# Non-local attention in a four-stage fp32 kernel: which operand of the weighting matmul is held in the array, and how the rows' sums are divided out

## What is computed

```python
s = xf * gate                                  # 256 channels x L
theta, phi, g = (w @ s + b for three 1x1 convolutions)   # 128 x L each
attn = softmax(einsum("nci,ncj->nij", theta, phi), axis=-1)   # L x L
nl = einsum("ncj,nij->nci", g, attn)           # 128 x L
out = s + out_w @ nl + out_b
```

## Time and profile before

| | us |
|---|---|
| median of 3 runs | 7601.4 |
| the profiled execution's own time | 7604.33 |
| its span, first to last instruction | 7602.3 |
| PE busy (matmuls) | 6744.9 |
| DVE busy | 6281.6 |
| ACT busy | 5777.6 |
| POOL busy | 5368.3 |

### The profile page before, as it was taken

How to read it: one execution, slowest core, us unless ns; L and a number is a source line. 1 busy time by engine, 2 the same in 40 slices (tenths; PEclk the granted TensorE clock), 3 DMA queues, 4 the chain that set the end, 5 groups by cost and what they waited for, 6 DMA issues and landing times. The chain is left out here.

```text
span 7602.3 us, 146480 instructions
## 1 busy us (share of the span) xinstructions
PE 6744.9 (89%) x42848; PEld 4630.3 (61%) x42848; DVE 6281.6 (83%) x9629; ACT 5777.6 (76%) x9092; POOL 5368.3 (71%) x3394
## 2 busy tenths in 40 slices
PE   5787889989779999999999999999999999999998
PEld 3555547767646666666666666666666666666666
DVE  3334664444549999999999999999999999999997
ACT  3545112222249999999999999999999999999997
POOL 2424000000039999999999999999999999999997
PEclk7898999999989999999999999999999999999998
DMA  2000000000020000000000000000000000000000
GB/s 67 25 17 26 1 1 0 0 1 0 0 61 10 1 1 1 1 1 2 10 1 1 1 1 1 2 27 1 1 1 1 1 2 2 4 4 4 4 4 6
DMA packets 75943, 56.06 MB, mean 7 GB/s; under 512 B 50776, under 2 KB 73464, under 8 KB 75032
## 3 DMA queue, kind: packets, MB, share of 16 engines
q1 hardware_dynamic: 72512, 53.88, 2.6%
q10 hardware_dynamic: 3288, 0.33, 0.0%
HBM read 37.80 MB, written 16.37 MB: 7 GB/s over the span
## 5 line engine op out<-in xcount | busy, mean ns | idle before, releaser
L1482 POOL TENSOR_TENSOR a_s<-a_s,a_v 128x784 f32<-128x784 f32 x1568 | 2915.3, 1859 | 301.8 <-ACT a_s L1693 281.8
L1518 PE MATMUL a_right_sides<-a_s,diag_d 128*128 128x392 f32 x6272 | 2284.6, 507 | 8.1 <-POOL a_s L1482 1.0
L1518 PEld LDWEIGHTS a_right_sides<-a_s,diag_d 128*128 128x128 f32 x6272 | 1132.1, 190 | 1052.1 <-POOL a_s L1482 309.0
L1614 DVE SCALAR_TENSOR_TENSOR a_kan<-a_s,spline_c,a_kan 128x784 f32<-128x784 f32 x1568 | 1621.3, 1034 | 50.4
L1541 PEld LDWEIGHTS a_weighed<-a_V,a_probT 112*128 112x128 f32 x10976 | 1375.5, 193 | 162.2
L1475 POOL TENSOR_TENSOR a_inner<-a_inner,a_x 128x784 f32<-128x784 f32 x784 | 1460.0, 1862 | 0.0
L1541 PE MATMUL a_weighed<-a_V,a_probT 112*128 112x65 f32 x10976 | 1366.3, 270 | 0.0
L1693 ACT ACTIVATE a_s<-a_v 128x784 f32<-128x784 f32 x1568 | 1335.3, 852 | 4.7
L1684 ACT ACTIVATE a_v<-a_a 128x784 f32<-128x784 f32 x1568 | 1336.1, 852 | 0.3
L1530 PE MATMUL a_turned<-ident,a_prob 128*112 128x128 f32 x5488 | 856.8, 278 | 229.9 <-ACT a_probT L1700 228.2
L1585 DVE TENSOR_SCALAR a_x<-a_scores 128x392 f32<-128x392 f32 x1568 | 874.5, 558 | 20.3 <-PE a_scores L1505 20.3
(11 more groups left out here) (176 smaller groups left out, 6818.9 us busy)
## 6 DMA issues: line engine op xcount, KB each, us to landing
rows<-bias_rows_dram SPq DMA_DIRECT2D x112, 91.0 KB
X<-in_x_dram SPq DMA_DIRECT2D x4, 1568.0 KB, 16.2
a_q<-q_dram SPq DMA_DIRECT2D x392, 16.0 KB, 2.0
mask<-in_window_mask_dram SPq DMA_DIRECT2D x56, 98.0 KB
v_dram<-V SPq DMA_DIRECT2D x14, 227.5 KB, 2.3
a_V<-v_dram SPq DMA_DIRECT2D x4, 796.2 KB, 9.2
q_dram<-Q SPq DMA_DIRECT2D x14, 224.0 KB, 1.9
k_dram<-K SPq DMA_DIRECT2D x14, 224.0 KB, 1.9
```

The source lines that it names most:

```text
L1482: eng.tensor_tensor(s, s, v, ALU.mult).then_inc(cubed, 1)
L1518: mm = eng.matmul(up[:, j, 0:SUB], steps[i][:, :], cubes[g][:, SUB * j:SUB * (j + 1)], start=(i == 0), stop=(i == 1))
L1614: eng.scalar_tensor_tensor(F, banked((s1, s2)[j][g][:, :]), c[:, 3 + j:4 + j], F, ALU.mult, ALU.add).then_inc(left_added, 1)
```

## The change

The weighting matmul swaps its operands: the values `gT` are stationary (112 rows, 128 columns) and the turned probabilities are moving (112 columns), so that `op` has channels on the partitions and queries along the columns, as `nl` has. `op` becomes two PSUM tiles used in turn, each with room for two pictures of 112 columns.

The sums are then needed per column. `normalise` on DVE makes `share`, the identity with each row multiplied by its reciprocal sum; `spread_shares` on PE, in `turn_out`'s place, multiplies a matrix of ones with it, which puts each query's reciprocal on all 128 partitions, into the second half of the `op` bank; and `keep_spread` on DVE copies that to SBUF (`spread`) and multiplies the output by it straight into `nl`. `keep_spread` has lag 2 and stands between `row_max` and `normalise`. `turn_out`, `o`, `otp` and ACT's `place_out` go. POOL sets the ones once in each call, ahead of its first query tile. PE's first weighting matmul of a tile waits for `o_placed` of the tile two before it, where it waited for `o_normed`.

```diff
@@ -1062,7 +1062,9 @@
         q = [sb(f"q{r}", [P, TILE]) for r in range(2)]
         prob = [sb(f"prob{r}", [TILE, L]) for r in range(2)]
         probT = [sb(f"probT{r}", [TILE, 4, TILE]) for r in range(2)]
-        o = [sb(f"o{r}", [TILE, P]) for r in range(2)]
+        share = [sb(f"share{r}", [TILE, TILE]) for r in range(2)]
+        ones = sb("ones", [TILE, P])
+        spread = sb("spread", [P, TILE])
         gmax = [sb(f"gmax{r}", [TILE, 4]) for r in range(2)]
         rmax = [sb(f"rmax{r}", [TILE, 1]) for r in range(2)]
         nmax = [sb(f"nmax{r}", [TILE, 1]) for r in range(2)]
@@ -1070,12 +1072,11 @@
         rinv = [sb(f"rinv{r}", [TILE, 1]) for r in range(2)]
         scp = [ps(f"scores{i}", [TILE, 2, 512]) for i in range(2)]
         tp = [ps(f"turned{i}", [TILE, 4, TILE]) for i in range(2)]
-        op = ps("op", [TILE, P])
-        otp = ps("otp", [P, TILE])
-
-
-        q_ready, s_made, s_copied, max_step, max_ready, exp_done, turned, copied_v, copied_a, pv_done, inv_ready, o_normed, o_turned, o_placed = (
-            sem(n) for n in ("q_ready", "s_made", "s_copied", "max_step", "max_ready", "exp_done", "turned", "copied_v", "copied_a", "pv_done", "inv_ready", "o_normed", "o_turned", "o_placed"))
+        op = [ps(f"op{r}", [P, 2, 256]) for r in range(2)]
+
+
+        q_ready, s_made, s_copied, max_step, max_ready, exp_done, turned, copied_v, copied_a, pv_done, inv_ready, ones_set, spread_kept, share_made, shares_spread, o_placed = (
+            sem(n) for n in ("q_ready", "s_made", "s_copied", "max_step", "max_ready", "exp_done", "turned", "copied_v", "copied_a", "pv_done", "inv_ready", "ones_set", "spread_kept", "share_made", "shares_spread", "o_placed"))
 
         def copied(c, t):
 
@@ -1095,6 +1096,7 @@
                 def stage_q(eng, t, r):
                     eng.wait_ge(s_made, 4 * (t + 1))
                     eng.tensor_copy(q[r][:, :], theta[:, bass.ds(TILE * t, TILE)]).then_inc(q_ready, 1)
+                pool.memset(ones[:, :], 1.0).then_inc(ones_set, 1)
                 pipeline(pool, TILES, [(stage_q, 0)])
 
             @block.tensor
@@ -1119,24 +1121,23 @@
                                 mm = eng.transpose(tp[(r + c) % 2][:, j, :], prob[r][:, at:at + TILE], m.ident[0:TILE, 0:TILE])
                             mm.then_inc(turned, 1)
                         if c == 1:
-                            eng.wait_ge(o_normed, t + 1)
+                            eng.wait_ge(o_placed, t + 1)
                         if c >= 1:
                             eng.wait_ge(*copied(c - 1, t))
                             for j in range(4):
                                 k = 4 * (c - 1) + j
-                                mm = eng.matmul(op[:, :], probT[(r + c - 1) % 2][:, j, :], gT[:, k, :], start=(k == 0), stop=(k == TILES - 1))
+                                mm = eng.matmul(op[r][:, 0, 0:TILE], gT[:, k, :], probT[(r + c - 1) % 2][:, j, :], start=(k == 0), stop=(k == TILES - 1))
                             mm.then_inc(pv_done, 1)
 
-                def turn_out(eng, t, r):
-                    eng.wait_ge(o_normed, t + 2)
-                    eng.wait_ge(o_placed, t + 1)
-                    eng.transpose(otp[:, :], o[r][:, :], m.ident[0:TILE, 0:TILE]).then_inc(o_turned, 1)
+                def spread_shares(eng, t, r):
+                    eng.wait_ge(share_made, t + 1)
+                    eng.matmul(op[r][:, 1, 0:TILE], ones[:, :], share[r][:, :], start=True, stop=True).then_inc(shares_spread, 1)
 
                 pe.sem_inc(s_made, 8)
                 pe.sem_inc(turned, 14)
                 pe.sem_inc(pv_done, 7)
-                pe.sem_inc(o_turned, 2)
-                pipeline(pe, TILES, [(scores, 0), (turn_out, 2), (values, 1)])
+                pe.wait_ge(ones_set, 1)
+                pipeline(pe, TILES, [(scores, 0), (spread_shares, 2), (values, 1)])
 
             @block.vector
             def _(dve):
@@ -1156,14 +1157,19 @@
                         copy_chunk(eng, eng.tensor_copy, t, r, c, copied_v)
                     eng.reciprocal(rinv[r][:, :], rsum[r][:, :]).then_inc(inv_ready, 1)
                     eng.wait_ge(inv_ready, t + 1)
-                    eng.wait_ge(pv_done, 7 * (t + 2))
-                    eng.wait_ge(o_turned, t + 1)
-                    eng.tensor_scalar(o[r][:, :], op[:, :], rinv[r][:, :], None, ALU.mult).then_inc(o_normed, 1)
+                    eng.tensor_scalar(share[r][:, :], m.ident[0:TILE, 0:TILE], rinv[r][:, :], None, ALU.mult).then_inc(share_made, 1)
+
+                def keep_spread(eng, t, r):
+                    eng.wait_ge(shares_spread, t + 1)
+                    eng.tensor_copy(spread[:, :], op[r][:, 1, 0:TILE]).then_inc(spread_kept, 1)
+                    eng.wait_ge(spread_kept, t + 1)
+                    eng.tensor_tensor(nl[:, bass.ds(TILE * t, TILE)], op[r][:, 0, 0:TILE], spread[:, :], ALU.mult).then_inc(o_placed, 1)
 
                 dve.sem_inc(s_copied, 2)
                 dve.sem_inc(copied_v, 4)
-                dve.sem_inc(o_normed, 1)
-                pipeline(dve, TILES, [(row_max, 0), (normalise, 1)])
+                dve.sem_inc(o_placed, 2)
+                pipeline(dve, TILES, [(row_max, 0), (keep_spread, 2), (normalise, 1)])
+                dve.wait_ge(o_placed, TILES + 2)
 
             @block.scalar
             def _(act):
@@ -1171,18 +1177,13 @@
                     for c in (1, 3, 5):
                         copy_chunk(eng, eng.copy, t, r, c, copied_a)
 
-                def place_out(eng, t, r):
-                    eng.wait_ge(o_turned, t + 3)
-                    eng.copy(nl[:, bass.ds(TILE * t, TILE)], otp[:, :]).then_inc(o_placed, 1)
-
                 def exponent(eng, t, r):
                     eng.wait_ge(max_ready, t + 1)
                     eng.activation(prob[r][:, :], prob[r][:, :], ACT.Exp, bias=nmax[r][:, :], accum_out=rsum[r][:, :]).then_inc(exp_done, 1)
 
                 act.sem_inc(copied_a, 3)
-                act.sem_inc(o_placed, 1)
-                pipeline(act, TILES, [(copies, 1), (place_out, 2), (exponent, 0)])
-                act.wait_ge(o_placed, TILES + 1)
+                pipeline(act, TILES, [(copies, 1), (exponent, 0)])
+                act.wait_ge(exp_done, TILES)
 
 
 def project_out2(nc, m, b, s, nl):
```

## The result

The changed kernel took 7642.71 us (median of 4 runs, 7639.53 to 7657.48), before 7601.47: ratio 1.0057, 95% interval 1.0046 to 1.0069. It is slower by 0.57% (0.54% between the medians); the forecast was 7630 us, +0.37%.

A forecast was written before the change was run, and what follows sets the result against it. Tile time in softmax2 was set by PE's pass rate and DVE's short chain inside PE's 1.34 us gap. Passes 6.0, keep_spread 21.8 and ones 0.6 summed to +28.4 us on 7601.4: 7630 us, range 7608 to 7652.

The forecast's parts named there:

- Pass pitch, +6.0 us: Weighting matmuls of softmax2: swapped operands cost +0.0019 us on each of 3136 passes, then at 0.1115 us; +6.0 us.
- A: Weighting passes: moving columns set the pitch, so 112 columns pass in 0.096 us; faster, 7581 us; chance 0.06.
- C: Weighting passes: weight load and pass take turns, 0.207 us a pass; +326 us, 7928 us; chance 0.03.
- keep_spread in the gap, +21.8 us: DVE, ahead of the chunk-0 copy PE waits for: +0.42 us in each of 52 steps, +21.8 us (19 to 40).
- Rival B: keep_spread is hidden because the chunk-0 copy awaits PE, not DVE; no measurable change, 7608 us; chance 0.09.
- the term was 30 us: keep_spread on DVE: by the skill's strict sentence its two joints cost 0.08 us more each, 52 x 0.58 = 30 us.
- What was costed at nothing: spread_shares' extra 0.12 us, hidden by PE's gap (7 us if uncovered); share, place_out's removal, two banks, o_placed: nothing.
- about 96 us: Sign of being right: PE's weighting wait for DVE's chunk-0 copies goes up from 73.8 to about 96 us.
- granted clock still 1.00 in both stretches: Sign of being right: TensorE keeps its full clock in both softmax2 calls; under 1.00 would be an unsummed cause.

The follow-up runs named there:

- e1: Changed kernel with keep_spread moved behind normalise in DVE's order and two spread buffers; 7597.44 us, ratio 0.9996.
- e4: Changed kernel with the chunk copies dealt the other way (ACT the even chunks, DVE the odd ones); 7557.05 us, ratio 0.9941.
- e6: Changed kernel with ACT copying the even chunks, DVE the odd ones, and keep_spread moved behind normalise; 7558.26 us, ratio 0.9944.
- e2: Kernel before the change, operands not swapped, with two dependent idle DVE instructions put between row_max and normalise; 7658.34 us, ratio 1.0072.
- e5: Changed kernel with four more unread matmuls on PE ahead of each tile's first weighting pass; 7626.71 us, ratio 1.0033.
- e7: Changed kernel measured again unaltered, five later runs; 7654.14 us, ratio 1.0070.

## Why the prediction came out as it did

The direction and the two places were right, and the first measurement lies in the range; but of the sum one term is right, one is some 5 us too small, and one is missing.

- *Pass pitch, +6.0 us.* e1 has +0.10 us a tile, 56 of them 5.6 us: right. The passes stand at 0.112 us. Rivals A and C fall with it. Where the Trainium skill (TensorE: Matmul & The Clock Gate, "The mechanism") lets a weight load overlap a running matmul only in another row group, the trace contradicts it: loads of 0.200 us (mean of the row above) and passes 0.112 us apart.
- *keep_spread in the gap, +21.8 us.* 16.58 - 16.055 = 0.525 us a tile between the changed kernel and e1, 27 us over 52: inside 19 to 40, mis-sized by the joint between copy and product, put at 0.04 and measured at 0.14. Rival B falls. By the strict sentence of the Trainium skill (VectorE: DVE Perf Modes, "The DRAIN you can't avoid") the term was 30 us, an estimate; but the spread copy starts at 1309.69, 0.08 us before the negation ends, and the chunk-0 copy at 1310.30, 0.08 before the product ends, so that is not what made it larger.
- *What was costed at nothing* shows no cost in this kernel: e1, which keeps all of it, has calls 4.2 us longer than before, no more than the pitch. The spreading matmul's 0.10 us a tile show only in e4 and e6, where its cover is gone. But the sign "about 96 us" for the weighting's wait left out that this matmul takes 6 us of that gap; the 94.9 measured are near it only because keep_spread cost 27.
- *The step that failed* is "granted clock still 1.00 in both stretches". It stood in the text as something that would make the prediction wrong, with no price: 15 drops, 25.2 us. A longer gap on PE was costed at its length alone; e1, e2 and e5 show that the gap brings the drops. Longer tiles (31.8) and drops (25.2) come to 57.0 us; the forecast had 28.4.
- That the measurement lies in the range is in part luck. The measured 41 us look closer to the forecast than they should: three of the first four runs lie at 7640 to 7645 us, and the profiled one of them (7640.41) ended at 0.90 of the clock (how the other two ended is not shown); the five of e7 lie at 7653 to 7656. With the end as in e7 the change costs 53 us, and 7654 is above the range's 7652.

## What to carry to other kernels

Before swapping matmul operands to save moving columns, read the pitch of a row in the new shape: in float32 the larger of stationary and moving columns set it here, so 112 under 128 gained nothing over 128 under 112. An instruction that may run at any time belongs behind the one that the bounding engine waits for: the order on DVE alone made 53 of the 57 us that the two calls grew by. And a stall of the matmul engine can cost more than its length where it brings the clock down, so after any such change read the granted clock of the stretch beside the gap.

## What was not expected of the hardware

A PE gap that went from 1.32 to 1.69 us in each tile of about 16 us brought 15 stretches of 3.4 us at half clock, each worth 1.7 us (25.2/15), at the same places in two profiles; filling the gap with work that nobody reads made the program 27 us faster. And an address that depends on a register cost about 0.1 us where it was computed behind a wait for the instruction just before (0.14 against 0.03 us, in one kernel).
